# Weighing two key tiles together, one group of output columns after the other, in an attention kernel

## What is computed

```python
q = jnp.einsum('bchw,oc->bohw', x, Wq).reshape(b, HEADS, dq, n)
k = jnp.einsum('bchw,oc->bohw', x, Wk).reshape(b, HEADS, dq, n)
v = jnp.einsum('bchw,oc->bohw', x, Wv).reshape(b, HEADS, dv, n)
attn = jax.nn.softmax(jnp.einsum('bhdn,bhdm->bhnm', q, k), axis=-1)
out = jnp.einsum('bhnm,bhdm->bnhd', attn, v)
...
return gamma * out + sc
...
x = x + _L0_conv_ref(_gn(x), L0_conv_Wq, L0_conv_Wk, L0_conv_Wv, L0_conv_Wsc, L0_conv_gamma)
```

## Time and profile before

| | us |
|---|---|
| median of 3 runs | 3241.45 (3241.27 to 3243.91) |
| the profiled execution | 3242.41 |
| its span, first to last instruction | 3240.7 |
| TensorE matmuls busy | 3151.1 |
| TensorE weight loads busy | 2149.4 |
| VectorE busy | 2203.3 |
| ScalarE busy | 2086.5 |
| GpSimd busy | 2767.2 |
| mean granted TensorE clock | 0.998 of full speed |

### The profile page before, as it was taken

One profiled execution on the slowest core, in us unless ns is written; L12 is line 12 of the kernel. 1 busy time (PEld: TensorE's weight loads), 2 busy tenths in 40 slices (PEclk: granted clock), 3 DMA queues, 4 the chain that ended last, 5 costly groups with the idle time before them and its releaser, 6 DMA issues.

```text
span 3240.7 us, 120165 instructions
## 1 busy us (share of the span) xinstructions
PE 3151.1 (97%) x52880; PEld 2149.4 (66%) x52880; DVE 2203.3 (68%) x3682; ACT 2086.5 (64%) x3443; POOL 2767.2 (85%) x2098
## 2 busy tenths in 40 slices
PE   5999999999999999999999999999999999999998
PEld 3666666666667666666666766666666666766665
DVE  7776666676677666676667766667666666666797
ACT  4666667766666666766666666677666666666665
POOL 2788989989898898988889888898888989889877
PEclk9999999999999999999999999999999999999999
DMA  3010001100011000110001100011000000000000
GB/s 125 24 36 22 17 22 37 31 22 17 22 36 41 17 12 27 31 44 14 12 27 41 36 12 17 22 46 32 15 14 14 15 14 15 12 17 12 17 17 15
DMA packets 53032, 82.68 MB, mean 26 GB/s; under 512 B 4384, under 2 KB 50464, under 8 KB 52512
## 3 DMA queue, kind: packets, MB, share of 16 engines
q1 hardware_dynamic: 52512, 74.99, 7.3%
HBM read 56.10 MB, written 18.87 MB: 23 GB/s over the span
## 4 chain that ended last, share of the span: by engine, by line
PE 65%; POOL 22%; issue 4%; DVE 4%; ACT 2%; POOLq 0%; DVEq 0%
POOL PLO L895 17%; PE SL L419 17%; PE PJ L350 13%; PE OB L439 9%; PE MX L391 8%; PE OB L442 7%; PE OB L441 6%; PE PJ L347 4%; POOL DF L875 2%; POOL QK L881 2%; ACT PE L542 1%; DVE mx L681 1%; DVE PLO L737 1%; DVE mx L678 1%; PE PJ L375 1%
## 5 line engine op out<-in xcount | busy, mean ns | idle before, releaser
L895 POOL TENSOR_TENSOR PLO<-PE 128x768 f16<-128x768 f32 (+1 forms) x1728 | 2474.3, 1455 | 409.5 <-ACT PE L542 401.1
L542 ACT ACTIVATE PE<-SL 128x768 f32<-128x768 f32 x1728 | 1310.6, 815 | 14.3 <-PE SL L419 14.3
L439 PEld LDWEIGHTS OB<-V,PE 128*128 128x128 bf16 x10368 | 949.4, 99 | 281.9 <-POOL PLO L895 152.7
L678 DVE TENSOR_REDUCE mx<-MX 128x1 f32<-128x384 f32 x864 | 481.0, 557 | 934.0 <-PE MX L391 932.7
L439 PE MATMUL OB<-V,PE 128*128 128x65 f16 x10368 | 1068.6, 194 | 25.4 <-POOL PLO L895 24.9
L441 PE MATMUL OB<-V,PE 128*128 128x64 f16 x10368 | 1059.0, 193 | 0.0
L442 PE MATMUL OB<-V,PLO 128*128 128x65 f16 x10368 | 1058.1, 196 | 0.0
L550 ACT ACTIVATE MXC<-MX 128x384 f32<-128x384 f32 x864 | 424.5, 491 | 941.1 <-PE MX L391 927.5
L419 PE MATMUL SL<-QK 64*128 64x384 f16 x10368 | 999.4, 323 | 0.0
L441 PEld LDWEIGHTS OB<-V,PE 128*128 128x128 bf16 x10368 | 966.2, 97 | 0.0
L442 PEld LDWEIGHTS OB<-V,PLO 128*128 128x128 f16 x10368 | 965.7, 98 | 0.0
(11 more groups left out here) (108 smaller groups left out, 1501.3 us busy)
## 6 DMA issues: line engine op xcount, KB each, us to landing
gx<-x SPq DMA_DIRECT2D x36, 768.0 KB, 4.5
xr<-x SPq DMA_DIRECT2D x96, 192.0 KB, 2.4
out<-xr SPq DMA_DIRECT2D x96, 192.0 KB, 1.9
X<-x SPq DMA_DIRECT2D x6, 768.0 KB, 8.8
QK<-wk SPq DMA_DIRECT2D x1, 1024.0 KB, 12.7
QK<-wq SPq DMA_DIRECT2D x1, 1024.0 KB, 13.4
QK<-wv SPq DMA_DIRECT2D x1, 1024.0 KB, 14.1
QK<-wsc SPq DMA_DIRECT2D x1, 1024.0 KB, 15.3
```

The lines of the kernel that those rows point to most:

```text
L439: pe.matmul(acc, upper, v[:, D:V1], start=k == 0 and h == 0 and i == 0, stop=False, skip_group_check=True)
L542: act.activation(PE32[:, s % PB, :].rearrange("p (h n) -> p h n", h=2), SL[s % 2][:, :, 0:CH], ACT.Exp, scale=1.0 / SS).then_inc(s_exp, 1)
L678: nc.vector.tensor_reduce(mx3[:, n % 2, 0, k:k + 1], MX[:, 0, 0:CH], AX.X, ALU.max).then_inc(s_mxf, 1)
L895: nc.gpsimd.tensor_tensor(PLO[:, s % PB, lo:], PE32[:, s % PB, lo:], PE32[:, s % PB, lo:].bitcast(BF16)[:, 1:2 * (2 * CH - lo):2], ALU.sub ...
```

## The change

`weigh` is taken apart into its waits (`weighable`) and the three matmuls of one tile for one group of output columns (`weigh_tile`). A new `weigh_two(s)` makes the waits of both tiles first. Then it goes through the 6 groups, and gives each the three matmuls of tile s and the three of tile s + 1 before it goes to the next. So a group gets six matmuls in a row. Turn 1 of each chunk, which weighs the first two tiles of the chunk, keeps the old order; the 8 others and the last pair of the kernel use the new one. Each tile's last matmul counts `s_av` up, so the first tile's count comes with its last group. The number of matmuls and weight loads stays the same.

```diff
--- before.py
+++ after.py
@@ -420,28 +420,46 @@
                                          start=False, stop=a == DH and b == QL, skip_group_check=True)
                 last.then_inc(s_score, 1)
 
-            def weigh(s):
+            def weighable(s):
+
                 n, k = divmod(s, MT)
-                g = n // NCH
                 if k == 0:
                     if n:
                         pe.wait_ge(s_oe, n)
-                    left(("v", g, NCH - 1))
+                    left(("v", n // NCH, NCH - 1))
                 pe.wait_ge(s_rest, s + 1)
                 if s >= LAST:
                     pe.wait_ge(s_restd, s - LAST + 1)
+
+            def weigh_tile(s, h, i):
+                n, k = divmod(s, MT)
+                p0 = h * CH + i * P
+                acc = OB[:, (h * QT + i) * OW:(h * QT + i) * OW + AW]
+                upper = PE32[:, s % PB, p0:p0 + P].bitcast(BF16)[:, 1:2 * P:2]
+                v = V[:, n // NCH % 2, k, h * V1:(h + 1) * V1]
+                pe.matmul(acc, upper, v[:, D:V1], start=k == 0 and h == 0 and i == 0, stop=False,
+                          skip_group_check=True)
+                pe.matmul(acc[:, 0:D], upper, v[:, 0:D], start=False, stop=False, skip_group_check=True)
+                last = pe.matmul(acc, PLO[:, s % PB, p0:p0 + P], v[:, D:V1], start=False,
+                                 stop=k == MT - 1 and h == 1 and i == QT - 1, skip_group_check=True)
+                if h == 1 and i == QT - 1:
+                    last.then_inc(s_av, 1)
+
+            def weigh(s):
+
+                weighable(s)
                 for h in range(2):
                     for i in range(QT):
-                        p0 = h * CH + i * P
-                        acc = OB[:, (h * QT + i) * OW:(h * QT + i) * OW + AW]
-                        upper = PE32[:, s % PB, p0:p0 + P].bitcast(BF16)[:, 1:2 * P:2]
-                        v = V[:, g % 2, k, h * V1:(h + 1) * V1]
-                        pe.matmul(acc, upper, v[:, D:V1], start=k == 0 and h == 0 and i == 0, stop=False,
-                                  skip_group_check=True)
-                        pe.matmul(acc[:, 0:D], upper, v[:, 0:D], start=False, stop=False, skip_group_check=True)
-                        last = pe.matmul(acc, PLO[:, s % PB, p0:p0 + P], v[:, D:V1], start=False,
-                                         stop=k == MT - 1 and h == 1 and i == QT - 1, skip_group_check=True)
-                last.then_inc(s_av, 1)
+                        weigh_tile(s, h, i)
+
+            def weigh_two(s):
+
+                weighable(s)
+                weighable(s + 1)
+                for h in range(2):
+                    for i in range(QT):
+                        weigh_tile(s, h, i)
+                        weigh_tile(s + 1, h, i)
 
 
             pe.wait_ge(s_const, 3)
@@ -484,9 +502,11 @@
                     score(n, 2 * m + 1)
                     if U < TOPS:
                         top(U + 1)
-                    if s:
+                    if s and m == 1:
                         weigh(s - 2)
                         weigh(s - 1)
+                    elif s:
+                        weigh_two(s - 2)
                     if m == 0 and n >= 2:
                         turn(n - 2)
                     u = slot_unit(n, m)
@@ -498,8 +518,7 @@
                         root(*root_unit(n, m)[1:])
                     if u and m % 2 == 0:
                         project(u, 4, 6)
-            weigh(STEPS - 2)
-            weigh(STEPS - 1)
+            weigh_two(STEPS - 2)
             turn(CHUNKS - 2)
             turn(CHUNKS - 1)
 
```

## The result

The changed kernel takes 3265.1 us (3264.6 to 3265.6), the kernel before in the same comparison 3241.8 us (3241.3 to 3243.9). The ratio is 1.007 (95% interval 1.0057 to 1.0083): slower by some 23 us, where 12 to 13 had been forecast.

What follows compares the result with a forecast made beforehand. TensorE bounds most turns, GpSimd the 45 stretches where it runs back to back. Part 1 (5.5 + 8 + 1.5 = 15 us), others 0, gave 3256 against the median, less 2: 3254 us, range 3235 to 3271.

Steps and rivals of the forecast that it cites:

- starvation: Rival, chance 0.10: GpSimd waits in turn 7 for exponentials, the stretch grows, nothing is absorbed in turn 1; 3271 us.
- Part 2: Order of output columns on TensorE: 6 of 11 group changes vanish in 768 turns; taken as 0, between 23 us gain and 10 loss.
- rival of a toll on the column group: Rival: each step to another column group costs 5 ns; 3237 us in full, 3246 at half; chance 0.25 together.
- the faster side: Rival, chance 0.12: steps within a group save over 5.5 ns or waits cost half as much; both a little better, 3231 us.
- remark on the 16 bytes: V's 516-byte tile starts at a multiple of 16 bytes in turn 6, not turn 7; read as cause of dear steps.
- Part 1: TensorE's wait for the second tile moves ahead of the first: main term, 15 us, bounds about 5 and 43 us.
- The lateness in turn 7: Chunk 42 to 43: the pair starts when tile 2 started before, 0.56 us late, containing turn 6's 0.36 us.
- The cover of GpSimd in turn 7: First exponential ends 0.49 us before GpSimd takes it, less 0.06 for the semaphore, against 0.36 lateness; if gone, 9 us more.
- plain stretches: GpSimd back to back from turn 5 to the next chunk's turn 1; 42 count, each keeping 0.13 us: 5.5 us.
- the three blocks with the group statistics: Blocks where 9 small chained GpSimd operations finish the statistics; lateness with no turn 1 behind it, 2.6 us each, 8 us.
- the last block: Where VectorE does part of the splitting: a few pairs late by less, 1 to 2 us, including the final pair's wait.
- The deduction of 2 us: Taken off the sum because lateness that meets TensorE's waits for VectorE's maxima is given back in part; leaves 3254 us.

## Why the prediction was right, and where its sum was short

*The direction and the mechanism* held. The forecast was 3254 us for 3265, inside the range of 3235 to 3271, from the wait of the second tile that moves ahead of the first. The run with the waits alone has the whole loss. The size was short: 3265 lies outside the narrower 3247 to 3260 that the prediction gave its own mechanism, and nearer to the 3271 of starvation.

*Part 2* (the order is worth 0) held, and its ground, the reads of V, held in the main. 35 changes of group for 11 cost nothing, and the padding takes away dear steps with the groups left as they were. But the prediction misread the pair of turns from which it drew this. It set the first head of turn 6 beside the second head of turn 7; in turn 6 too the second head steps dearly into a new group (1507.38 to 1507.42 us). The heads differ in their start: the last six matmuls of a head's nine take 179 ns where its part of V starts at a multiple of 16 bytes, 182 to 183 at other multiples of 4, and 187 to 189 off a multiple of 4. The rival of a toll on the column group falls, and with it the faster side that rested on it. The prediction's remark on the 16 bytes was worth more than the change: padding alone gives 0.5%. The Trainium skill ("SBUF — State Buffer", Specifications (TRN2)) gives SBUF 16-byte cachelines, with a penalty for each crossing to a new one. A row of 64 columns fills 8 such lines at an aligned start and touches 9 at any other, and the order of the runs (129 elements 3242 us, 130 elements 3233, 136 elements 3226) goes the same way. It can't be the whole account. By the same lines (an estimate) a row of 65 columns, 130 bytes, touches 9 at every even start, so that one read of three gains by an aligned start; and with 130 elements most reads still start off a multiple of 16, yet more than half of the gain is there. The page says nothing of why a start off 4 bytes should be dearer than one off 16, which the trace shows.

*Part 1*, 15 us before the small deduction, measured 23. The step that failed is its first number: "a semaphore takes some 0.06 us", read from a wait in front of tile 2 and carried over to the pair. The trace before couldn't show the new place, but the listing of the change could have told that two waits now stand in a row. That is a term that the sum didn't have: 90 ns at each late pair, 10 us in all by the run with one wait. The Trainium skill ("Perfetto Trace Analysis", Identifying Dependency Chains) says that an instruction that waits on several engines may get EventSemaphore instructions put ahead of it. The trace has 864 of them for 96 at the weighing; it shows them for two waits on one engine's count too, of which the page doesn't speak, and it adds the price.

It acted in three places. The lateness in turn 7 is 0.67 for 0.56. 78 turns, most of them turns 6 and 8 of chunks 3 to 5, had started their pair 73 to 117 ns after the second split's end; they now start 145 ns after it, 4.5 us later in all. And the cover of GpSimd in turn 7, "it just fits", no longer did: between the two pairs of splits lie 0.92 us (1519.19 to 1520.11), for 0.84 before (1510.51 to 1511.35). That is the starvation's sign, idle time of GpSimd before its splits, and turn 8's 0.81 us of lateness holds it. So a tenth of a microsecond per stretch is the starvation rival's, in small. With one wait the measured 3255.3 us lie 1.3 us above the forecast: the missing term is this one. That they lie so near is in part luck. Traced from start to start, the blocks with plain stretches alone cost 2.4 us in that run where 5.5 were forecast, the three blocks with the group statistics 6.4 for 8, and the last block 4.3 for 1.5; another 1.6 us lie ahead of the first weighing, where nothing was changed.

*The other terms.* From start to start over all turns the stretches lost 31 us in turns 6 to 8 and 0 (25 forecast) and got 19 back in turn 1 (19 to 20 forecast). The blocks with the group statistics lost 3.0 us each (2.6 forecast), the last block 5 (1 to 2 forecast). In its turns the partner is late by little and often, and the wait for VectorE's part keeps its own instruction in every run: it still lost 4.3 us with one wait and 2.7 with the wait behind the first matmul. How much of the 5 us are the 90 ns stays open.

*A sign that could not tell.* The prediction would have taken a pair of 1.12 us or less for a toll. Unhindered pairs take 1117 ns in the changed kernel, but 1124 in the kernel before and 1117 with the waits alone: the mark was set from turn 7, a dear one.

*The deduction of 2 us* for waits on VectorE's maxima stays undecided: with one wait, 3255.3 us lie between the sums with it (3254) and without (3256).

## What to carry to other kernels

A wait that has work of its own engine in front of it is cheaper than the same wait moved ahead of that work, even if few turns wait for that input (280 of 864 here); before joining two steps, list which input of the second is late and what covers it. Put two waits on one count into one: the later value implies the earlier, and a second wait in a row is an instruction of its own on the critical path. Where two different counts must be waited for, the last block suggests to write the wait first that ends last; no run tests that order. And where short matmuls keep a pace that is some nanoseconds dearer than their columns, try the start addresses of the moving operand before the order of the outputs.

## What the runs showed of the hardware that I had not expected

- Two waits in a row ahead of a weight load: 145 ns from the end of the releasing instruction to the matmul where the wait that got its own instruction ends last, for 56 ns with one wait or where the weight load's own wait ends last. The passage from 64-row to 128-row matmuls adds nothing behind a wait.
- Matmuls of 64 and 65 columns of 16-bit data step at 29 ns, with about every third step at 33 to 36 ns where reads start off a multiple of 16 bytes; in turns in which neither they nor the instruction after them wait, 36 take 1124 ns on average with rows of 516 bytes, 1106 with 520 and 1093 with 544.
- Where three matmuls in a row read the same columns of V, each for another group of outputs, most of what padding brings to the pace is there without it (1102 ns for the 36), and 10 of the 16 us.
- A step of 35 ns about every sixth matmul stays with aligned reads, and leaving out one column in three matmuls doesn't remove it. Its cause was not found.
